# Batch attention with routing: steps reordered, two band copies on ScalarE's queue, second offset row added by VectorE

## The reference

```python
def _moe(x, Wg, W1, b1, W2, b2):
    xf = x.reshape(S * B, D)
    logits = xf @ Wg.T
    idx = jnp.argmax(logits, axis=-1)
    ...
        h = jax.nn.relu(xf @ W1[e] + b1[e])
        out = out + m * (h @ W2[e] + b2[e])
y = _layer_norm(x + _mha(x, Wqkv, bqkv, Wo, bo), g1, be1)
z = _layer_norm(y + _moe(y, Wg, W1, b1, W2, b2), g2, be2)
```

## Time and profile before

| what | before |
|---|---|
| median of 3 runs (lowest to highest) | 999.71 us (999.56 to 1000.05) |
| profiled execution, its own time | 999.7 us |
| its span, mean granted TensorE clock | 997.9 us, 0.924 |
| busy over the span: PE, DVE, ACT, POOL | 838.0, 825.3, 605.8, 707.4 us |
| stage of the change, 638 to 819 us: PE, DVE, ACT, POOL | 129.2, 143.9, 96.4, 124.6 us of 181.0 |
| expert stage, 834 to 997.9 us: PE, DVE | 144.6, 140.4 us of 163.9 |

### The profile page before, as it was taken

How to read it: one execution, slowest core, us unless ns; L and a number is a source line. 1 busy time by engine, 2 the same in 40 slices (tenths; PEclk the granted TensorE clock), 3 DMA queues, 4 the chain that set the end, 5 groups by cost and what they waited for, 6 DMA issues and landing times. The chain is left out here.

```text
span 997.9 us, 21606 instructions
## 1 busy us (share of the span) xinstructions
PE 838.0 (84%) x5240; PEld 616.6 (62%) x5240; DVE 825.3 (83%) x2581; ACT 605.8 (61%) x1556; POOL 707.4 (71%) x450
## 2 busy tenths in 40 slices
PE   5599999999969959999999997289887715999993
PEld 5456666666647736666666664156565505999993
DVE  5569999999958957999999998569798743999995
ACT  2656656665349945676665753377664105999992
POOL 4489999999835538999999997364997460455554
PEclk9899999999979979999999999599999556999997
DMA  9430000000000000000000000544767564544410
GB/s 252 160 88 1 1 2 1 1 1 1 1 4 1 1 1 1 12 22 16 18 22 11 22 22 22 155 118 127 205 207 210 170 202 135 142 130 134 132 57 18
DMA packets 64972, 70.54 MB, mean 71 GB/s; under 512 B 8965, under 2 KB 52178, under 8 KB 64740
## 3 DMA queue, kind: packets, MB, share of 16 engines
q1 hardware_dynamic: 50612, 47.20, 17.1%
q0 software_dynamic: 6368, 16.89, 5.0%
q10 hardware_dynamic: 7872, 5.08, 2.0%
HBM read 32.32 MB, written 24.50 MB: 57 GB/s over the span
## 5 line engine op out<-in xcount | busy, mean ns | idle before, releaser
L484 PE MATMUL a_pS<-a_kv,utri 128*128 128x360 f32 (+3 forms) x768 | 262.8, 479 | 14.9 <-POOL a_kv L474 13.6
L474 POOL TENSOR_TENSOR a_kv<-a_qk,a_vv 128x2304 f32<-128x2304 f32 (+1 forms) x64 | 253.9, 3968 | 13.8 <-DVE a_qk L445 13.5
L579 DVE TENSOR_TENSOR a_tt<-a_pS,a_qk 128x360 f32<-128x360 f32 (+3 forms) x384 | 188.6, 526 | 24.2 <-PE a_pS L484 22.6
L484 PEld LDWEIGHTS a_pS<-a_kv,utri 128*128 128x128 f32 x768 | 139.6, 192 | 96.4 <-POOL a_kv L474 23.2
L596 POOL TENSOR_TENSOR a_tt<-a_tt 128x1152 f32<-128x1152 f32 (+1 forms) x64 | 146.7, 2292 | 28.4 <-DVE a_tt L579 28.3
L2105 POOL DMA_INDIRECT out_dram<-x_o,x_place x71 | 69.4, 977 | 77.1 <-DVE x_o L2092 75.1
L607 DVE TENSOR_REDUCE a_nd<-a_tt 128x144 f32<-128x720 f32 (+3 forms) x128 | 101.5, 814 | 0.4 <-POOL a_tt L596 0.3
L1685 POOL DMA_INDIRECT ys<-m_S,m_dest x64 | 63.2, 987 | 35.1 <-issue 13.3
L544 ACT ACTIVATE a_tt<-a_pI 128x144 f32<-128x144 f32 (+1 forms) x96 | 40.1, 417 | 70.1 <-PE a_pI L496 68.4
L2043 PE MATMUL x_pZ<-w,x_hT 128*128 x568 | 76.3, 278 | 1.5 <-issue 1.4
L418 ACT ACTIVATE a_vv<-a_pQ 128x128 f32<-128x128 f32 x122 | 33.9, 278 | 66.1 <-PE a_pQ L409 65.9
(11 more groups left out here) (303 smaller groups left out, 2136.3 us busy)
## 6 DMA issues: line engine op xcount, KB each, us to landing
x_yl<-ys SPq DMA_DIRECT2D x71, 193.5 KB, 2.5
X<-xs SPq DMA_DIRECT2D x16, 256.0 KB, 5.3
kx<-m_kc SPq DMA_DIRECT2D x64, 64.0 KB
ax<-m_pc SPq DMA_DIRECT2D x64, 64.0 KB
m_S<-X SPq DMA_DIRECT2D x16, 256.0 KB, 3.1
xs<-X SPq DMA_DIRECT2D x15, 256.0 KB
w<-in_L_ffn_W_dram SPq DMA_DIRECT2D x1, 2048.0 KB
m_S<-gw ACTq DMA_DIRECT2D x6, 256.0 KB, 3.0
```

What stands on the lines that cost most here:

```text
L474: pool.tensor_tensor(kv[:, t:t + 2, :, :, :].rearrange("p t h j i -> p (t h) j i"), kk.unsqueeze(2).to_broadcast([P, 2 * H, J, D]), rows.u ...
L484: pe.matmul(pS[c][:, 0:(h1 - h0) * SC], K.utri[:, :], flat[:, h0 * SC:h1 * SC], start=True, stop=True).then_inc(u_done, 1)
L579: v.tensor_tensor(tt[:, t, h0:h1, :, 0:D], pS[c][:, 0:(h1 - h0) * SC].rearrange("p (h j i) -> p h j i", i=D, j=J), q[:, h0:h1, :].unsqueez ...
```

## The change

The row gb is added to x by DVE at the end of a step (vec_xb), no longer by POOL. POOL's step is two scatters, product, two scatters, addition. The four band copies ax are split: SP issues bands 0 and 1 at the start of its step, ahead of keys and x, ACT bands 2 and 3 at the end of its own; each waits for the transposition of the same step. vec_choose is cut into pieces that are interleaved with the softmax: a piece signals the chain semaphore (done) and the next piece waits for it (last) only when it comes to run. The scan reads its table from PSUM, where a copy (vec_choose_carry) puts it in each even step. The destinations are interleaved with the statistics. PE projects v ahead of q and k, and ACT's copies follow another order.

```diff
+        ramp = pS[:, 256:256 + 9 * E]
...
-        def pool_xb(pool, g):
-
-            pool.wait_ge(xn_ready, 4 * g + 4)
-            pool.wait_ge(gate_done, 1)
+        def vec_xb(v, g):
+
+            v.wait_ge(xn_ready, 4 * g + 4)
+            v.wait_ge(gate_done, 1)
             x = K.X[:, ds(4 * g, 4), :]
-            pool.tensor_tensor(x, x, over(gb[:, :]), ALU.add).then_inc(xb_ready, 1)
+            v.tensor_tensor(x, x, over(gb[:, :]), ALU.add).then_inc(xb_ready, 1)
 
...
+            pe.wait_ge(hT_ready, g + 1)
...
-            wait(v, hot_ready, (g - 2) // 2)
...
-        def sp_ax(sp, g):
-
-            sp.wait_ge(pc_ready, g + 1)
-            wait(sp, o_ps, g - 1)
-            for c in range(4):
+        def ax_bands(q, g, bands):
+
+            q.wait_ge(pc_ready, g + 1)
+            wait(q, o_ps, g - 1)
+            for c in bands:
                 rows = slice(32 * c, 32 * c + 32)
-                sp.dma_start(ax[rows, g % 2, c, :], pc[rows, g % 2, :, :].rearrange("p a s -> p (a s)"))\
-                  .then_inc(ax_in[g % 2], 16)
+                q.dma_start(ax[rows, g % 2, c, :], pc[rows, g % 2, :, :].rearrange("p a s -> p (a s)"))\
+                 .then_inc(ax_in[g % 2], 16)
 
...
+        def vec_choose_logits(v, done, last, r):
 
             n = tiles(r)
-            ties = tie[:, :].unsqueeze(1).to_broadcast([P, n, E])
-            lgn, mine = lg[:, 0:n, :], hot[:, :, 1:1 + n].rearrange("p e n -> p n e")
             v.wait_ge(lg_ready, groups(r)[-1] + 1)
             v.wait_ge(rstd_done, r + 1)
-            wait(v, pos_ps, r)
             v.wait_ge(sm_ready, min(2 * r + 5, G))
-            if r == G // 2 - 1:
...
+        def vec_choose_carry(v, r):
+
+            v.wait_ge(sm_ready, min(2 * r + 5, G))
+            v.tensor_copy(ramp, reset[:, :, :].rearrange("p e n -> p (e n)")).then_inc(ramp_done, 1)
...
+        def vec_choose_hot(v, done, last, r):
+
+            n = tiles(r)
+            last()
+            wait(v, pos_ps, r)
+            if r == G // 2 - 1:
+                done(v.memset(hot[:, :, 5:9], 0.0))
+            done(v.tensor_tensor(hot[:, :, 1:1 + n].rearrange("p e n -> p n e"), tie[:, :].unsqueeze(1).to_broadcast([P, n, E]),
+                                 by_e(first[:, 0:n], n), ALU.is_equal))
...
+        def vec_choose_scan(v, last, r):
+            last()
+            v.wait_ge(ramp_done, r + 1)
+            v.tensor_tensor_scan(upto[:, :, :].rearrange("p e n -> p (e n)"), ramp,
...
             if there(s + 2):
+                pe_v(pe, s + 2)
                 pe_qk(pe, s + 2)
-                pe_v(pe, s + 2)
...
+            if there(s + 4):
+                act_xn(act, s + 4)
+            if there(s):
+                act_exp(act, s)
+            if there(s + 2):
+                act_v(act, s + 2)
+            if there(s - 2):
+                act_places(act, s - 2)
+            if there(s + 2):
+                act_q(act, s + 2)
+            if s == G - 1 or s == G:
+                act_rstd(act, s - 9)
+            if there(s - 1):
+                act_o(act, s - 1)
+            if there(s + 2):
+                act_k(act, s + 2)
+            if there(s + 3):
+                act_hT(act, s + 3)
+            if s in PARTS:
+                act_stats(act, *part_of(s))
+            if even(s - 3) and s < G - 1:
+                act_rstd(act, (s - 3) // 2)
+            if there(s):
+                ax_bands(act, s, (2, 3))
...
+        def vec_step(v, s, done, last):
+
+            choice = (s - 4) // 2 if even(s - 4) and s < G else None
+            place = (s - 5) // 2 if even(s - 5) and s < G else None
             if there(s - 2):
                 vec_u(v, s - 2)
+            if place is not None:
+                vec_dest_pick(v, place)
+            if there(s - 2):
+                vec_stats(v, s - 2, (0,))
+            if place is not None:
+                vec_dest_sum(v, done, place)
+            if there(s - 2):
                 vec_logits(v, s - 2)
-                vec_stats(v, s - 2)
-            if even(s - 5) and s < G:
-                vec_dest(v, link, (s - 5) // 2)
+                vec_stats(v, s - 2, (1,))
+            if place is not None:
+                vec_dest_cast(v, last, place)
             if there(s):
                 vec_max(v, s)
+            if there(s - 2):
+                vec_stats(v, s - 2, (2,))
+                vec_stats(v, s - 2, (3,))
+            if there(s):
                 vec_shift(v, s)
             if there(s - 2):
-                vec_var(v, s - 2)
+                vec_var(v, s - 2, (0, 1))
             x_stats(v, s)
             if s in PARTS:
                 v.wait_ge(stats, 4 * (PARTS[s][2] - 2))
                 vec_x_var(v, *part_of(s))
-            if even(s - 4) and s < G:
-                vec_choose(v, link, (s - 4) // 2)
+            if place is not None:
+                vec_dest_carry(v, done, place)
+            if there(s - 2):
+                vec_var(v, s - 2, (2, 3))
+            if choice is not None:
+                vec_choose_logits(v, done, last, choice)
+                vec_choose_mean(v, choice)
+                vec_choose_offset(v, done, last, choice)
+                vec_choose_carry(v, choice)
+                vec_choose_best(v, done, last, choice)
             if there(s):
                 vec_total(v, s)
+            if choice is not None:
+                vec_choose_equal(v, done, last, choice)
+            if there(s):
                 vec_reciprocal(v, s)
+            if choice is not None:
+                vec_choose_ties(v, done, last, choice)
+                vec_choose_first(v, done, last, choice)
+            if there(s):
                 vec_probs(v, s)
+            if choice is not None:
+                vec_choose_hot(v, done, last, choice)
+            if there(s):
                 vec_transpose(v, s)
+            if choice is not None:
+                vec_choose_scan(v, last, choice)
             if s in PARTS:
                 vec_x_offset(v, *part_of(s))
+            if there(s + 3):
+                vec_xb(v, s + 3)
...
             if there(s - 5):
                 pool_row(pool, s - 5, 0)
+                pool_row(pool, s - 5, 1)
             if there(s + 4):
                 pool_scale(pool, s + 4)
             if there(s - 5):
-                pool_row(pool, s - 5, 1)
+                pool_row(pool, s - 5, 2)
+                pool_row(pool, s - 5, 3)
             if there(s + 4):
                 pool_h(pool, s + 4)
-            if there(s - 5):
-                pool_row(pool, s - 5, 2)
-            if there(s + 3):
-                pool_xb(pool, s + 3)
-            if there(s - 5):
-                pool_row(pool, s - 5, 3)
 
...
                 def sp_step(sp, s):
+                    if there(s):
+                        ax_bands(sp, s, (0, 1))
                     if there(s + 2):
                         sp_kx(sp, s + 2)
                     if there(s - 2):
                         sp_xb(sp, s - 2)
-                    if there(s):
-                        sp_ax(sp, s)
 
...
-                def link(ins):
+                def done(ins):
 
                     count[0] += 1
                     ins.then_inc(chain, 1)
-                    v.wait_ge(chain, count[0])
+
+                def last():
+
+                    wait(v, chain, count[0])
+
+                def link(ins):
+
+                    done(ins)
+                    last()
 
                 v.tensor_tensor(gb[:, :], K.rows[:, 3, :], K.tab[:, 2, :], ALU.mult).then_inc(gate_done, 1)
 
```

More of the change, by code:

```diff
@@ L1588, in vec_logits, with vec_stats, vec_var @@
              .then_inc(lg_ready, 1)
-        def vec_stats(v, g):
+        def vec_stats(v, g, ts=range(4)):
             v.wait_ge(u_ready, g + 1)
             wait(v, var_done, 4 * g)
-            for t in range(4):
+            for t in ts:
                 v.bn_stats(ubn[:, t, :], S[:, 4 * (g % RG) + t, 0:P]).then_inc(bn_done, 1)
-        def vec_var(v, g):
+        def vec_var(v, g, ts=range(4)):
             v.wait_ge(bn_done, 4 * g + 4)
@@ L1632, in vec_choose, with vec_choose_mean @@
+        def vec_choose_carry(v, r):
+            v.wait_ge(sm_ready, min(2 * r + 5, G))
+            v.tensor_copy(ramp, reset[:, :, :].rearrange("p e n -> p (e n)")).then_inc(ramp_done, 1)
+        def vec_choose_mean(v, r):
+            v.wait_ge(rstd_done, r + 1)
             v.scalar_tensor_tensor(out=S[:, pair(r), MR], in0=umv[:, half(r), 0], scalar=-1.0, in1=S[:, pair(r), RS],
                                    op0=ALU.mult, op1=ALU.mult).then_inc(mr_done, 1)
-            link(v.tensor_tensor(lgn, raw[:, half(r), :], by_e(S[:, pair(r), RS], n), ALU.mult))
@@ new lines, in vec_choose_best, with vec_choose_equal, vec_choose_ties @@
+        def vec_choose_best(v, done, last, r):
+            n = tiles(r)
+            last()
+            done(v.tensor_reduce(best[:, 0:n], lg[:, 0:n, :], AX.X, ALU.max))
+        def vec_choose_equal(v, done, last, r):
+            n = tiles(r)
```

(47 more changed lines are left out.)

51 lines of the change are left out of this document (11 added, 40 removed).

## The result

| what | before | changed |
|---|---|---|
| median (lowest to highest) | 999.63 us (998.82 to 1000.05) | 990.68 us (988.72 to 992.12) |
| changed / before, 95% interval | | 0.9912, 0.9889 to 0.9934 |
| profiled execution, its span | 999.7, 997.9 us | 991.3, 989.5 us |
| busy over the span: PE, DVE, ACT, POOL | 838.0, 825.3, 605.8, 707.4 us | 839.7, 821.7, 603.8, 687.8 us |

Forecast were 989.9 us with a range from 985.0 to 996.5 and 0.92 for faster; the median lies 0.8 us beside it. To compare stages I cut each trace at four marks: DVE's product m_gb, with which the stage begins, the transpositions of steps 4 and 12, and the start of the last scatter.

A forecast was written before the change was run, and what follows sets the result against it. With PE, DVE and POOL near 90% busy in the batch attention stage, their order and locks were taken to decide. Gains of 6.7 + 0.5 + 2.6 = 9.8 us took 999.7 to 989.9 us, range 985.0 to 996.5.

The forecast's parts named there:

- The bound: Steps 5 to 12: a pair of steps takes 15.6 us, POOL's 15.0 plus a cast delay; 6.7 us gained.
- The rival of the light lock: DVE's additions hardly held by POOL: a pair takes 14.5 to 15.0 us, time 986.4; chance 17%.
- A: Second offset row moved to DVE: POOL's pair 15.0 us, from 17.4; DVE gets 1.2 us more per pair.
- I had set 5% on that: Slower rival: DVE's additions held 1.75 us twice a pair, 18.3 us against 17.3, time 1003.6; chance 5%.
- B: Choice interleaved on DVE: 11 or 12 of 17 dependent pairs broken up, 1.3 us saved per pair of steps.
- E: Bands first on SP, two of four on ACT: last band 1.2 us earlier; later keys and ACT issues called free.
- C: Ramp in PSUM: one more copy, 0.1 us per pair; scan at 0.31 us, its 1.75 us hold gone.
- D: PE projects v before q and k: PE's loop is 14.5 us per pair, which cannot be beaten.
- The first steps as a whole: Steps -4 to 4: 0.5 us gained, bounds -1 and +1.5.
- the rival that this makes ACT late: Slower issues on ACT delay normalisation and exponential 0.5 us in 12 steps, or keys come late: 995.5 us; chance 16%.
- The tail: Steps 13 to 15: gains of 0.7, 0.9 and 1.0 us, 2.6 in all, bounds 1 and 4.

The follow-up runs named there:

- sp_pads_cast: Changed kernel with gate and pad copies issued by SP instead of ACT, and the sums the cast reads in PSUM for units 0 to 5; 988.42 us.
- c_only: Kernel before with one edit: the scan reads its table from a copy in PSUM; 996.47 us, ratio 0.9985.
- a_only: Kernel before with only the offset additions at the end of DVE's step and the changed kernel's order on POOL; 1001.93 us, ratio 1.0030.
- no_b: Changed kernel with the choice and the destinations as one block each on DVE, not interleaved; 994.40 us, ratio 0.9960.
- no_c: Changed kernel with the scan reading its ramp from SBUF again, the copy into PSUM kept; 990.10 us, ratio 0.9924.

## Why the prediction held, step by step

**The bound.** Right: POOL's step is 7.5 us, and a pair on POOL is 15.0 plus the wait for the cast (715.15 to 730.80, 15.65 us), as said; 61.89 us against the forecast 62.4. The rival of the light lock had half of its mechanism right, the additions were never held, but the cast was (0.92 to 1.41 us in three pairs), and so its 14.5 to 15.0 per pair came only with sp_pads_cast. Of the kernel before, the prediction read a hold of 2.1 us in each pair of the middle. The scan was held 0.36 and 0.94 us in the first two pairs and 1.75 only in the last two, and c_only shows that these holds cost next to nothing: the 17.4 us of POOL's pair were the bound. Two sums of the rivals are slightly off as written: 10 + 0.5 + 2.6 is 13.1 and not 13.3, and 989.9 + 6 is 995.9 and not 995.5. Both stay inside the range.

**A.** Right in size and incomplete in reason. The prediction gave the 2.4 us of POOL's pair; a_only shows that the same edit gives back 1 us per pair and more where DVE's additions begin in the wrong scatter. I had set 5% on that. The prediction had not worked out in which scatter the end of DVE's step falls; that it fell in a harmless one was luck as far as its reasoning goes. Which of B to E keeps it out of the wrong one is open: with any single one of them taken back the additions stayed free (one in no_b, begun inside POOL's addition, took 0.85 us), with all of them (a_only) they did not; that is a matter of several edits together, and I did not try pairs of them.

**B.** -1.3 us of DVE per pair was forecast, 5.2 in four; the four pairs lost 3.3 to 3.4 us without it. A reading that fits, though not tested apart: with B POOL's pair of 15.65 us is the longer one, and what DVE saves beyond that shows nowhere.

**C.** The size of the scan was right, 0.27 to 0.31 us in all nine, and the reason given not needed. The prediction let the hold of 1.75 us go because the scan keeps one SBUF operand; no_c has two and is not held. In the order of before the ramp in PSUM did take the hold away (c_only), but for 0.4 us, since POOL was the bound.

**D.** "14.5 us per pair, from u to u" bounded nothing in the end. What PE's order does in the changed kernel is to save 4 us in the first steps, a place where the prediction had no term for it. It is no gain against before: ACT's new order takes v first, and D keeps PE in step with it. The first steps as a whole gained 0.12 in place of 0.5 us. One loss there that I had not seen is ACT's exponential of step 1, for which DVE waits 1.1 us: two bands, a gate copy and the normalisation stand ahead of it.

```profile
666.42 1.65 ACT L1406 ACTIVATE m_xn<-X,nmr,rstd 128x128 f32<-128x128 f32 x4
667.97 0.61 ACT L1513 ACTIVATE m_ex<-m_sm 128x512 f32<-128x512 f32 x1
```

**E.** The two issues took 1.43 us on ACT in the even steps from 2 on, not 1.2 (1.18 to 1.36 in the odd ones from 5 to 13); the rival that this makes ACT late was seen in single steps, and cost something only where the cast no longer set the pace. The Trainium skill (Trainium Kernel Development and Optimization, Key Constraints) has it that a second queue saves issue time alone; no run here shows more than that.

**The tail.** 2.14 us against 2.6. From the transposition of step 12 the output matmuls of group 14 came 2.57 us earlier than before, which is the sum forecast, but not by its terms: the values of group 12 gave 0.25 us and not 0.7, and nearly all the rest came in step 14, where the wait of group 14's values for their bands went from 2.53 to 0.43 us. POOL's last 21 scatters then took 26.0 us and not 25.6 (one waits 0.78 us for values matmuls, where 0.30 is fixed), which took 0.4 back.

**The start of the stage**, 1.0 us later than in the trace of before, is no part of the change: in its second profile the changed kernel had it at 638.66, before at 638.74.

## What to carry to other kernels

When two engines hold each other back, the share of time in which one is busy didn't tell the cost here; what stood behind the instruction in which the other began did. The order of four scatters and two products or additions on POOL was worth 7 us with nothing else changed, and an edit that is worth 5 us of the stage beside the others cost 2 by itself; so read the phase of each pair from a timeline before moving work to the freed engine.

When parts of a change are taken back one at a time, their losses need not add up to the gain: without A, B or D the stage was 5.0, 5.0 and 4.5 us longer, 14.5 together, where the whole change gained 9.5. D's part is no gain against before at all; it undoes a loss that ACT's new order would bring. And a hold may hide the next limit behind it: taken away alone it gave nothing, with the gate and pad copies moved off ACT's queue as well it gave 1.9 us.

## What the runs showed of the hardware

From 14 traces (before, the changed kernel and the twelve runs), DVE's instructions that begin between 690 and 765 us, by what POOL does at their start. "Held" is over 0.25 us beyond their free duration. In the middle column the product or addition starts less than 0.1 us after the scatter's end.

| DVE instruction | in a scatter, product or addition straight behind | in a scatter, another scatter behind |
|---|---|---|
| offset addition, 2 SBUF operands (0.65 us free) | 7 of 7 held, by 1.23 to 1.66 us | 0 of 62 |
| scan, 2 SBUF operands (0.27) | 5 of 5, by 1.55 to 1.80 | 0 of 4 |
| cast, SBUF to SBUF (0.15) | 9 of 11, by up to 1.45 | 0 of 5 |
| carry copy, SBUF to SBUF (0.14) | 5 of 6, by up to 1.46 | 0 of 36 |
| u addition, one operand in PSUM (0.68) | 0 of 25 | 0 of 41 |
| scan, ramp in PSUM (0.27) | 0 of 8 | 0 of 25 |
| transposition, one operand (0.71) | 0 of 20 | 0 of 11 |

A scatter by itself does not hold DVE. One that POOL's next product or addition follows without a gap does, already before that product begins and until it ends. This covers the last part of the scatter and not the whole of it: the 26 held ones began 0.02 to 0.61 us ahead of the product or addition, the three free ones 0.78 to 0.94 us ahead. c_only has one of each kind, casts begun 0.26 us before POOL's addition at 728.98 and 0.86 us before that at 746.41:

```profile
728.72 1.60 DVE L1668 CAST m_dest<-m_posf 128x8 uint32<-128x8 f32 x1
...
745.55 0.17 DVE L1668 CAST m_dest<-m_posf 128x8 uint32<-128x8 f32 x1
```

That DVE's instruction merely ran into POOL's does not explain it: the first cast, 0.17 us when free, would have been done by 728.89. Instructions of the first four rows that began inside a product or addition (35 of them, not in the table) never ended before it did.

The Trainium skill (SBUF — State Buffer, Who interferes with whom) says that who issues first gets the shared ports for the whole instruction; in the twelve cases of the first two rows DVE began first and was blocked. In five of them its lead was only 0.02 to 0.03 us, too little to say much; in the other seven it was 0.36 to 0.61 us. What POOL holds in that scatter these runs do not show. Another sentence of the Trainium skill in the same section, that a DVE instruction with at most one SBUF input outside the two-port modes does not contend, agrees with the last three rows.

Two DMAs took 1.43 us to issue on ACT's queue in the even steps of the changed kernel from 2 on, and 1.18 to 1.36 us in the odd ones from 5 to 13; on SP's they took 1.16 us in nearly every step.

```profile
711.24 1.43 ACTq L1544 DMA_DIRECT2D ax<-m_pc  x2
```
```profile
711.24 1.16 SPq L1544 DMA_DIRECT2D ax<-m_pc  x2
```
